# Weighted sum of the experts' results by TensorE with diagonal matrices, and the norm's small operations in another order

## What is computed

```
v        = (x - mean(x)) / sqrt(var(x) + 1e-5)
topk_p   = two best of sigmoid(v @ wa), divided by their sum   # the shares
routed   = sum over the two chosen experts of share * expert(v)
shared   = two experts that see every token
x        = x + v + shared + routed
```

## Time and profile before

| | us |
|---|---|
| median of 3 runs | 969.54 (968.85 to 970.51) |
| the profiled execution, its own time | 969.79 |
| its span | 968.5 |
| PE busy | 879.2 (91% of the span) |
| DVE busy | 717.4 (74%) |
| ACT busy | 596.9 (62%) |
| POOL busy | 589.9 (61%) |

### The profile page before, as it was taken

One profiled execution on the slowest core, in us unless ns is written; L12 is line 12 of the kernel. 1 busy time (PEld: TensorE's weight loads), 2 busy tenths in 40 slices (PEclk: granted clock), 3 DMA queues, 4 the chain that ended last, 5 costly groups with the idle time before them and its releaser, 6 DMA issues.

```text
span 968.5 us, 23186 instructions
## 1 busy us (share of the span) xinstructions
PE 879.2 (91%) x9330; PEld 731.1 (75%) x9330; DVE 717.4 (74%) x1287; ACT 596.9 (62%) x970; POOL 589.9 (61%) x603
## 2 busy tenths in 40 slices
PE   8799999999999999999999898899689888888992
PEld 6578788878888888888788886788566447676981
DVE  4788889788888987897888758643594877357744
ACT  4888877787787687777876541453497345241551
POOL 4895698678677876886786844423338641332342
PEclk9999999999999999999999999999899899899997
DMA  4321212021112111121110393963012112462644
GB/s 124 112 76 65 73 45 88 34 77 56 65 56 78 45 67 56 45 88 34 44 56 2 96 259 115 312 230 132 11 44 68 22 30 55 131 172 94 237 153 164
DMA packets 68417, 89.79 MB, mean 93 GB/s; under 512 B 11570, under 2 KB 49494, under 8 KB 68310
## 3 DMA queue, kind: packets, MB, share of 16 engines
q1 hardware_dynamic: 63062, 77.81, 25.1%
q0 software_dynamic: 3072, 8.39, 2.8%
q10 hardware_dynamic: 2176, 2.10, 0.6%
HBM read 59.57 MB, written 8.52 MB: 70 GB/s over the span
## 4 chain that ended last, share of the span: by engine, by line
PE 57%; DVE 24%; POOL 5%; ACT 5%; issue 5%; DMA 2%; another core or an unknown queue 0%; ACTq 0%; DVEq 0%; POOLq 0%; SPq 0%
PE psum L826 21%; DVE arena L1945 7%; PE psum L1125 5%; PE psum L798 5%; PE psum L909 4%; PE psum L901 4%; PE psum L954 3%; PE psum L1139 2%; DVE arena L1982 2%; PE psum L1263 1%; DVE v L2378 1%; PE psum L1297 1%; PE psum L1227 1%; DVE arena L2001 1%; DMA arena<-scratch_y 1%
## 5 line engine op out<-in xcount | busy, mean ns | idle before, releaser
L826 PE MATMUL psum<-vT,split 128*128 128x512 f32 x1368 | 343.1, 400 | 7.9 <-DVE arena L1945 5.5
L1945 DVE SCALAR_TENSOR_TENSOR arena<-psum,arena 128x1023 f32<-128x1023 f32 (+2 forms) x208 | 265.7, 1278 | 74.0 <-ACT arena L1454 51.4
L826 PEld LDWEIGHTS psum<-vT,split 128*128 128x128 f32 x1368 | 248.8, 188 | 63.6 <-DVE arena L1945 7.6
L1454 ACT ACTIVATE arena<-psum,arena 128x512 f32<-128x512 f32 x160 | 109.1, 690 | 66.2 <-PE psum L826 65.6
L1471 ACT ACTIVATE arena<-arena 128x1024 f32<-128x1024 f32 x80 | 84.2, 1058 | 34.9 <-POOL arena L2557 23.3
L2530 POOL TENSOR_TENSOR split<-arena,split 128x256 fp32r<-128x256 f32 x114 | 83.6, 742 | 30.7 <-ACT split L1381 30.6
L2557 POOL TENSOR_TENSOR arena<-arena,v 128x1021 f32<-128x1021 f32 x32 | 76.3, 2386 | 41.8 <-DVE arena L1945 41.8
L798 PE MATMUL psum<-ident,arena 128*128 128x128 f32 x568 | 73.0, 274 | 9.8 <-POOL arena L2587 6.1
L798 PEld LDWEIGHTS psum<-ident,arena 128*128 128x128 f32 x568 | 63.9, 140 | 21.3 <-POOL arena L2587 9.7
L1125 PE MATMUL psum<-arena,vT 128*128 x496 | 67.0, 278 | 3.4 <-issue 1.9
L1125 PEld LDWEIGHTS psum<-arena,vT 128*128 128x128 f32 x496 | 60.3, 192 | 6.5 <-issue 6.3
(11 more groups left out here) (283 smaller groups left out, 1733.9 us busy)
## 6 DMA issues: line engine op xcount, KB each, us to landing
bcast<-scratch_a SPq DMA_DIRECT2D x32, 512.0 KB, 3.7
vT<-arena SPq DMA_DIRECT2D x62, 256.0 KB
arena<-in_w_a SPq DMA_DIRECT2D x16, 768.0 KB, 4.2
arena<-in_wout_a SPq DMA_DIRECT2D x8, 256.0 KB, 2.6
scratch_v<-v SPq DMA_DIRECT2D x8, 256.0 KB, 5.2
arena<-scratch_y ACTq DMA_DIRECT2D x8, 256.0 KB, 5.2
arena<-scratch_y SPq DMA_DIRECT2D x8, 256.0 KB, 5.3
arena<-in_wg SPq DMA_DIRECT2D x4, 512.0 KB, 5.9
```

The source lines that it names most:

```text
L826: m = pe.matmul(bank, split[:, t % SPLITS, i, q, :], vT[:, j, q, half * BANK:(half + 1) * BANK], start=(n == 0), stop=(n == 3 * KD - 1))
L1454: act.activation(tile[:, hs], wide_of(t)[:, hs], ACT.Identity, scale=w[:, TAPS - 1:TAPS], bias=0.0).then_inc(sem["tap0"], 1)
L1945: dve.scalar_tensor_tensor(out=tile[:, s:T], in0=bank[:, 0:T - s], scalar=cw_a[:, j, i, TAPS - 1 - s:TAPS - s], in1=tile[:, s:T], op0=ALU. ...
```

## The change

Three things change.

1. **Both ends of the experts.** ACT writes for each chunk and choice a diagonal matrix, the identity times the token's share (`diagonals`, 16 of 128x128, in the buffers `bcast0` and `bcast3`), eight before it issues its loads of `scratch_y` and eight after. PE, behind its last `turn_out` and 45 fills, multiplies these with `y_e`: four matmuls of 128x256 in fp32 per quarter (`combine`), summed in PSUM, and then does 10 more fills. DVE adds one 128x512 sum per quarter to x. The 45 fills that stood in norm 2 are the same as those that now stand in front of the combining; the 5 and 5 between its quarters are gone.
2. **Statistics.** Norm 2 uses `layer_norm` in place of `layer_norm_paced`: the statistics of quarters 0 to 2, `low` 0, the statistics of quarter 3, then the other `low`s.
3. **-mean.** In all four norms it is computed by ACT, right ahead of each `norm_v`, and not by POOL.

```
-BUSY_NORM = ((12, 4, 4, 0), (5, 5, 5, 0), (45, 5, 5, 0), (5, 5, 5, 0))
+BUSY_NORM = ((12, 4, 4, 0), (5, 5, 5, 0), (0, 0, 0, 0), (5, 5, 5, 0))
+BUSY_BOTH = (45, 10)
...
                 if k == 2:
-                    on.wait_ge(sem["x_sh"], NC // 2)
+                    on.wait_ge(sem["x_out"], q + 1)
...
+                def combine(q):
+
+                    on.wait_ge(sem[f"yl{q}"], 16 * CHOICES * (n + 1))
+                    on.wait_ge(sem["diag"], 2 * n + q // 2 + 1)
+                    on.wait_ge(sem["x_sh"], NC // 2 * (n + 1))
+                    for c in (2 * q, 2 * q + 1):
+                        for i in range(CHOICES):
+                            m = pe.matmul(both_banks[q][:, c % 2 * D:(c % 2 + 1) * D], diag_e[i][:, c], y_e[:, i, c, :],
+                                          start=(i == 0 and c % 2 == 0), stop=(i == CHOICES - 1), skip_group_check=True)
+                    m.then_inc(sem["both"], 1)
...
+                on.wait_ge(sem["blk_hid"], BLOCKS * (n + 1))
+                keep_busy(up_banks[1], BUSY_BOTH[0])
+                for q in range(NC // 2):
+                    combine(q)
+                keep_busy(up_banks[1], BUSY_BOTH[1])
...
             def norm_v(k, q):
 
+                cs = slice(2 * q, 2 * q + 2)
+                on.wait_ge(sem["ln_mean"], NC * k + 2 * q + 2)
+                act.activation(nbias[:, cs], bn2[:, cs, 0], ACT.Copy, scale=-1.0).then_inc(sem["ln_neg"], 1)
                 on.wait_ge(sem["ln_bias"], NC // 2 * k + q + 1)
...
+                def diagonals(half):
+
+                    on.wait_ge(sem["router"], n_router(n, "parts"))
+                    on.wait_ge(sem["blk_up"], BLOCKS * (n + 1))
+                    for c in range(4 * half, 4 * half + 4):
+                        for i in range(CHOICES):
+                            m = act.activation(diag_e[i][:, c], ident[:, :], ACT.Identity, scale=share[:, i, c:c + 1],
+                                               bias=0.0)
+                    m.then_inc(sem["diag"], 1)
...
             def add_experts(n, q):
 
-                on.wait_ge(sem[f"yl{q}"], 16 * CHOICES * (n + 1))
-                on.wait_ge(sem["router"], n_router(n, "parts"))
+                cs = slice(2 * q, 2 * q + 2)
+                on.wait_ge(sem["both"], NC // 2 * n + q + 1)
+                on.wait_ge(sem["res"], NC // 2 * n + q + 1)
                 on.wait_ge(sem["x_sh"], NC // 2 * n + q + 1)
-                for i in range(CHOICES):
-                    for c in (2 * q, 2 * q + 1):
-                        if i:
-                            on.wait_ge(sem["x_y"], NC * n + c + 1)
-                        dve.scalar_tensor_tensor(out=x[:, c, :], in0=y_e[:, i, c, :], scalar=share[:, i, c:c + 1],
-                                                 in1=x[:, c, :], op0=ALU.mult, op1=ALU.add).then_inc(
-                                                     sem["x_out" if i else "x_y"], 1)
+                dve.tensor_tensor(x[:, cs, :], both_banks[q].rearrange("p (c d) -> p c d", c=2), x[:, cs, :],
+                                  ALU.add).then_inc(sem["x_out"], 1)
...
-            layer_norm_paced(2, experts_done)
+            layer_norm(2, experts_done)
...
-                pool.tensor_scalar(nbias[:, cs], bn2[:, cs, 0], -1.0, None, ALU.mult).then_inc(sem["ln_eps"], 1)
-                on.wait_ge(sem["ln_eps"], NC * k + 2 * q + 2)
+                on.wait_ge(sem["ln_eps"], NC // 2 * k + q + 1)
...
                 on.wait_ge(sem["ln_rstd"], NC // 2 * k + q + 1)
+                on.wait_ge(sem["ln_neg"], NC // 2 * k + q + 1)
```

More of the change, by code:

```diff
@@ L366 @@
  wb0 cb nw dskip ci_st ci0 ci1 ci2 mv0 mv1 mv2
- const zero ln_stat ln_mean ln_eps ln_rstd ln_v ln_hi unit proj dve_done act_done hi split narrow
+ const zero ln_stat ln_mean ln_eps ln_neg ln_rstd ln_v ln_hi unit proj dve_done act_done hi split narrow
  tap0 tap term light silu z decay decay_act expo expo_sel expd ud state square sq_sum nrm normed decay_pool nar_zero ln_bias
- tables pads biasT biasT_s owned owned_s ringw0 ringw1 ringw2 ringw3 ringw4 ringw5 ringw6 ringw7 gelu hid down router res x_sh x_y x_out ranked marked listed
+ tables pads biasT biasT_s owned owned_s ringw0 ringw1 ringw2 ringw3 ringw4 ringw5 ringw6 ringw7 gelu hid down router res x_sh diag both x_out ranked marked listed
  blk_t blk_ht blk_up blk_gelu blk_hid blk_dn blk_y blk_o blk_r blk_w
@@ L497, in hybrid_block @@
         ring_up = vT[:, :, :, :].rearrange("p i k t -> p (i k t)").bitcast(F32).rearrange("p (r n) -> p r n", r=UPS)
+        diag_e = [bcast[i].rearrange("p (c r) -> p c r", c=NC) for i in (0, 3)]
+        both_banks = [psum[:, i * BANK:(i + 1) * BANK] for i in range(4, 8)]
         ring_down = bcast[2].rearrange("p (r n) -> p r n", r=RING)
@@ L772, in sync_program @@
             for q in range(NC // 2):
-                on.wait_ge(sem["x_out"], NC + 2 * q + 2)
+                on.wait_ge(sem["x_out"], NC // 2 + q + 1)
                 sp.dma_start(io["out"][2 * q * P:(2 * q + 2) * P, :].rearrange("(c p) d -> p c d", c=2),
@@ L832, in narrow_half @@
                 bank = open_bank(units[half])
+                if k == 2:
+                    on.wait_ge(sem["x_out"], NC // 2)
                 if half == 0:
@@ L1657, in experts @@
                         block_out(j - 1, at[(j - 1) % GROUPED])
+                diagonals(0)
                 for r in range(RING):
@@ L1661, in experts @@
                     act.dma_start(y_e[:, 1, 2 * q:2 * q + 2, :], result_rows(1, q)).then_inc(sem[f"yl{q}"], 16)
+                diagonals(1)
             def second_layer():
@@ L1825, in layer_norm @@
                     low(k, q)
[L1827 to L1836, removed]
             def add_out(units):
@@ L2488, in experts_done @@
                     add_experts(0, c // 2)
-                on.wait_ge(sem["x_out"], c + 1)
+                on.wait_ge(sem["x_out"], c // 2 + 1)
             def second_done(c):
```

## The result

The changed kernel takes 980.99 us (median of 6 runs, 977.29 to 984.52), the kernel before 969.22 us (6 runs, 965.25 to 970.51). The ratio is 1.0118, with a 95% interval of 1.0097 to 1.0139. The profiled execution took 980.94 us where before's took 969.79. Repeated later, it was 1.0114 (1.0089 to 1.0139). The forecast was 978.8 us with a range of 974.3 to 981.8.

The account below looks back on a forecast made before the run. It took the second end as bound by loads and DVE's adds, the first by v 0 with its transposes and v 3. Terms -0.7 + 1.3 + 4.8 + 0.6 + 3.3 = +9.3 gave 979.1 profiled, 978.8 us median, range 974.3 to 981.8.

Parts of the forecast that it names:

- The second end: Second run's end: combining starts only when PE's 45 fills end, so the last add comes 3.3 us later.
- upper bound: Slowest sum of all terms, +13.3 us (982.8), with 3.6 us at the second run's end.
- The first end: First run's end into norm 2: fills, combining, later v 3 and six fills at half rate cost 4.8 us.
- half clock through norm 2: Rival, chance 0.14: norm 2 costs 6.6 in place of 4.8 us, more in norm 3; about +11.5, 981.
- The diagonals: Eight diagonals ahead of ACT's loads at the second end: estimated 2.4 us of ACT's time, cost taken as 0.
- The negation: ACT's negation behind the rounding: norm 0 gains 0.7 us, norm 1 loses 1.3, norm 3 loses 0.6.
- the negation hides: Rival, chance 0.17: ACT negates while it waits, norms 0, 1 and 3 gain 0.9, 0.3, 0.3; +5.6, 975.1.
- Statistics first: Norm 2: POOL's 4.05 us idle goes, but ACT's and POOL's loop ends last instead; v 3 1.9 us later.
- The sum: All five terms over the kernel: -0.7 + 1.3 + 4.8 + 0.6 + 3.3 = +9.3 us.
- the likeliest case: The whole kernel as forecast, 978.8 us, own range 976.5 to 980.5, chance 0.58.

Follow-up runs that it names:

- run 0: Not a follow-up: the first of the kernel's two runs of experts, ahead of the first end; 91.12 us before and 92.37 us changed in the first profiles.
- e10: The changed kernel, unchanged, profiled once more: 976.29 us, ratio 1.0114 to the kernel before.
- e12: The changed kernel, unchanged, profiled a third time: 979.48 us in one run.
- e4: The changed kernel with 34 fills ahead of combining and none behind, in place of 45 and 10: 972.72 us, ratio 1.0071 to the kernel before.
- e1: The changed kernel with the negation (-mean) back on POOL: 973.92 us, ratio 1.0078 to the kernel before.
- e2: The changed kernel with ACT's negation of the next quarter moved ahead of the rounding: 970.75 us, ratio 1.0064 to the kernel before.
- e6: The kernel before with only statistics first in norm 2 (layer_norm in place of layer_norm_paced): 964.17 us, ratio 1.0007.
- e9: The kernel before, unchanged, profiled once more: 963.97 us, ratio 0.9992.
- e3: The changed kernel with DVE's adds back at both ends, without diagonals, combining or fills behind it: 967.5 us, ratio 0.9984 to the kernel before.
- e7: e3 with the negation ahead of the rounding as in e2: 967.39 us, ratio 0.9982 to the kernel before.

## Why the prediction was right

**The second end** came as worked out. Combining began with the end of the 90 records, 6.91 us long (6.93 forecast), with the loads in, and the end took 17.68 us (17.9). The size was +3.07 against the profile that the sum was made from (+3.3), and +3.6 against the mean of three, since in that profile a load was late: that the term fits so well owes something to luck. The 3.6 us that the upper bound has for this end had no working behind it.

**The first end** was +4.8 in the sum; measured +4.35 in the first profile and +4.9 as a mean. With run 0 ending 1.64 us later, the forecast's marks stand at 688.8 for the transposes of quarter 0 (688.58), 693.4 for v 1 (692.88), 696.1 for v 2 (695.81), 697.7 for v 3 (697.37) and 702.0 for the wide product (701.56). Six fills at half rate were counted at 1.36 us more; they cost 1.2. POOL no longer idled for DVE between the quarters, and v 3 followed v 2 by 1.56 us (1.6 forecast). The narrow product ran at full rate in the first profile, 1.63 us, and almost so in e10, 1.75; in e12 and e4 it ran at or near half rate, 2.55 and 2.80. The Trainium skill (TensorE: Matmul & The Clock Gate, The HAM clock gate) has the throttled clock as the default state, which activity releases; as the prediction applied that, the narrow product would be at half rate, and the traces bear it out in some executions and not in others. So the rival "half clock through norm 2" is not another cause but another draw: the changed kernel had it in one of three profiles, and it added 1.05 us there, not 1.8.

**The diagonals** cost nothing, as taken: the first eight took 2.44 us and were done at 961.6, ahead of the loads' issue at 963.0, and the other eight at 968.3, ahead of combining at 969.7. The estimate worked out from the figures of the Trainium skill (ScalarE: Activation LUTs, What ACT_TABLE_LOAD costs) was 2.4 us, and the trace agrees.

**The negation** was -0.7, +1.3 and +0.6 in norms 0, 1 and 3; measured -0.70, +1.24 and +0.64 in the first profiles. As means, norm 3's term is +0.9: before's first profile had an unusually long norm 3 (12.25 us, then 11.98 and 11.99), so the fit of the +0.6 is in part luck. e1 shows that nothing else is in these terms, and e2 that the rival "the negation hides" fails by the order alone: where the negation stands ahead of the rounding, it does hide.

**Statistics first** were said to be eaten by ACT's and POOL's loop in the changed kernel. e6 shows that they are worth little even alone: 1.2 us of the 4 that v 3 was late.

**The sum** was +9.3; the same five stretches gave +8.6 in the first pair of profiles and +10.0 as means. What the prediction had no term for is the 1 to 2 us more in the medians; the unedited stretch that differs is layer b, +3.0 as a mean of three, whose length goes with the granted clock. So the mechanism and its size held, and where the last 1 to 2 us come from stays open. The result lies 0.5 us above the likeliest case's own range, 976.5 to 980.5.

## What to carry to other kernels

A cheap engine is not cheap where its queue is held: before moving a reduction to PE, read what stands ahead of it in PE's order (here 45 fills that were harmless while what came behind them wasn't ready) and when its operands land; fewer fills alone got 2.5 us back at one end and 2.9 at the other (e4). A small operation moved to another engine costs its place in that engine's order: 0.2 us cost 0.5 us a quarter behind the rounding, nothing ahead of it, and some 2 us when it was put ahead of work that needn't wait for its operand. Profile a kernel of this length more than once, and learn which stretches repeat: layer b moved by up to 3.2 us between executions of one kernel, the norms by less than 0.4, so a difference of 3 us is a finding in the one and may be nothing in the other.

## What the runs showed of the hardware

The same piece of layer b ran at either clock in different kernels: these two windows of 10 us lie 20 and 50 us behind the first wide product, first in e9, then in e3.

```profile
712.78:722.78 10.00, 8.53 (x39) 5.65 (x40) 9.61 (x10) 8.52 (x15) 6.11 (x4) 1.00 0.29 98
742.78:752.78 10.00, 7.72 (x142) 3.26 (x140) 9.26 (x11) 3.91 (x9) 7.73 (x6) 0.83 0.19 29
```

```profile
713.37:723.37 10.00, 9.75 (x38) 6.97 (x39) 9.60 (x10) 8.07 (x13) 6.11 (x4) 0.83 0.29 97
743.37:753.37 10.00, 6.47 (x142) 2.86 (x141) 9.64 (x11) 4.13 (x9) 7.86 (x6) 1.00 0.18 30
```

A window's clock is the mean over its 10 us. With nearly the same records PE is busy 8.53 us at a granted clock of 1.00 and 9.75 at 0.83 in the first, 7.72 at 0.83 and 6.47 at 1.00 in the second. All three executions of before and of the changed kernel lost the clock in the second piece and not in the first; e3, e6 and e7 the other way round, and e4 lost it in both. That a shift of a microsecond ahead of layer b decides where the clock falls in it is a guess that no run here tested. The median of the kernel before was 964.5 to 969.2 us on four occasions, two of them on one chip (964.5 and 968.95), and single runs of it lay between 958.7 and 974.1 us.
